# Loading a 1 MB weight table from a channel-major layout: 128 rows of 8 KB in place of 2048 runs of 512 B

## The chip, the cores and the metric

The kernel runs on one core of one Trainium2 chip. The metric is the device time of one execution in microseconds (us); lower is better. The median of three runs of the kernel before is 327.18 us (326.92 to 327.31).

## The reference

x holds 64 batches of 128 channels by 2048 time steps in fp32 (1 MB per batch). Each batch has a condition, an integer from 0 to 15, which picks one of 16 weight matrices of 128 x 128. The batch is multiplied by the picked matrix over its channels, and the product is added to the batch.

```
B, C, T = (64, 128, 2048)
S, D = (16, 128)
W = weights[condition]                       # (64, 128, 128)
out = x + jnp.einsum('bct,bcd->bdt', x, W)
```

The weights come as (state, channel, feature), S x C x D, 1 MB in all.

## The kernel before

A batch is one tile: channels on the 128 partitions, 2048 columns. SBUF holds a ring of 16 such tiles (x_ring: RING_TURNS 4 times STEPS 4), the table of all 16 matrices (weight_table, one row of 16 x 128 numbers per channel), four small tiles for the matrices in use (chosen_weights), and the conditions in one row. PSUM holds two products of four banks each. The order is written out by hand: each engine runs its own loop over turns of four batches and steps on semaphores.

- SyncE (SP) loads x, one DMA of 1 MB per batch (L63). It issues four at once; then load k+4 waits until load k has landed (L72, L76), and from the fifth turn on also until the store of batch k-12, which used the same ring tile, has landed (L77).
- ScalarE (ACT) first issues the load of the conditions (L138) and that of the weight table (L140), then stores one batch per DMA (L134). A store waits for the sum of its batch (L133) and for the landing of the store four batches before (L146). So at most four loads and four stores are under way.
- GpSimd (POOL) waits for both the conditions and the whole table (L89, L90). For each batch it reads the condition into a register and copies the picked 128 x 128 block out of the table into one of the four small tiles (L85). From the fifth batch on it waits until the product that used the tile before is done.
- TensorE (PE) waits for the batch and for its weights (L102, L103), and for the sum that frees its half of PSUM, and makes the product with four fp32 matmuls of 512 columns (L105), which the trace shows as eight instructions.
- VectorE (DVE) adds the product to the x tile in place (L127).

In the table load (L140) the partition is the channel. In memory a channel's data lies in 16 places, one per state, each 128 numbers or 512 B long and 64 KB from the next. The function kernel() makes the arrays contiguous on the host and launches.

Of the kernel before, what the change touches and what calls it, by code (L numbers as in the profile page):

```python
# [1 line left out]

# [3 lines left out]

BANK_COLUMNS = 512
PSUM_BANKS = 8
STEPS = 4
RING_TURNS = 4  # L20


def conditioned_residual(nc, x, condition, weights, out):
    fp32 = mybir.dt.float32
    batches, channels, time = x.shape
    states, _, features = weights.shape
    turns = batches // STEPS
    matmuls = time // BANK_COLUMNS
    psum_slots = PSUM_BANKS // matmuls

    with ExitStack() as ctx:
        def sbuf(name, shape, dtype=fp32):
            return ctx.enter_context(nc.sbuf_tensor(name, shape, dtype))

        def sem(name):
            return ctx.enter_context(nc.semaphore(name))

        x_ring = sbuf("x_ring", [channels, RING_TURNS * STEPS * time])
        weight_table = sbuf("weight_table", [channels, states * features])
        chosen_weights = [sbuf(f"chosen_weights{u}", [channels, features]) for u in range(STEPS)]  # L40
        condition_row = sbuf("condition_row", [1, batches], condition.dtype)
        product = ctx.enter_context(nc.psum_tensor("product", [features, psum_slots, time], fp32))


        condition_loaded = sem("condition_loaded")
        table_loaded = sem("table_loaded")
        x_loaded = [sem(f"x_loaded{u}") for u in range(STEPS)]
        out_stored = [sem(f"out_stored{u}") for u in range(STEPS)]

        weights_chosen = sem("weights_chosen")  # L50
        product_done = sem("product_done")
        sum_done = sem("sum_done")

        def ring_column(turn, u):

            return (turn % RING_TURNS) * (STEPS * time) + u * time

        block = ctx.enter_context(nc.Block())

        @block.sync  # L60
        def _(sp):
            def load(turn, u):
                sp.dma_start(x_ring[:, bass.ds(ring_column(turn, u), time)],  # L63
                             x[bass.ds(turn * STEPS + u, 1)].rearrange("b c t -> c (b t)")
                             ).then_inc(x_loaded[u], 16)

            for u in range(STEPS):
                load(0, u)

            with sp.Fori(1, RING_TURNS) as turn:  # L70
                for u in range(STEPS):
                    sp.wait_ge(x_loaded[u], 16 * turn)  # L72
                    load(turn, u)
            with sp.Fori(RING_TURNS, turns) as turn:
                for u in range(STEPS):
                    sp.wait_ge(x_loaded[u], 16 * turn)  # L76
                    sp.wait_ge(out_stored[u], 16 * (turn - RING_TURNS + 1))  # L77
                    load(turn, u)

        @block.gpsimd  # L80
        def _(pool):
            def choose(turn, u):
                state = pool.value_load(condition_row[0:1, bass.ds(turn * STEPS + u, 1)],
                                        min_val=0, max_val=states - 1)
                pool.tensor_copy(chosen_weights[u][:, :],  # L85
                                 weight_table[:, bass.ds(state * features, features)]
                                 ).then_inc(weights_chosen, 1)

            pool.wait_ge(condition_loaded, 16)  # L89
            pool.wait_ge(table_loaded, 16)  # L90
            for u in range(STEPS):
                choose(0, u)
            with pool.Fori(1, turns) as turn:
                for u in range(STEPS):

                    pool.wait_ge(product_done, (turn - 1) * STEPS + u + 1)
                    choose(turn, u)

        @block.tensor
        def _(pe):  # L100
            def multiply(turn, u):
                pe.wait_ge(x_loaded[u], 16 * (turn + 1))  # L102
                pe.wait_ge(weights_chosen, turn * STEPS + u + 1)  # L103
                for m in range(matmuls):
                    last = pe.matmul(product[:, u % psum_slots, m * BANK_COLUMNS:(m + 1) * BANK_COLUMNS],  # L105
                                     chosen_weights[u][:, :],
                                     x_ring[:, bass.ds(ring_column(turn, u) + m * BANK_COLUMNS, BANK_COLUMNS)],
                                     start=True, stop=True)
                last.then_inc(product_done, 1)

            for u in range(STEPS):
                if u >= psum_slots:
                    pe.wait_ge(sum_done, u - psum_slots + 1)
                multiply(0, u)
            with pe.Fori(1, turns) as turn:
                for u in range(STEPS):
                    pe.wait_ge(sum_done, turn * STEPS + u - psum_slots + 1)
                    multiply(turn, u)

        @block.vector  # L120
        def _(dve):
            with dve.Fori(0, turns) as turn:
                for u in range(STEPS):
                    tile = x_ring[:, bass.ds(ring_column(turn, u), time)]

                    dve.wait_ge(product_done, turn * STEPS + u + 1)
                    dve.tensor_tensor(tile, product[:, u % psum_slots, :], tile,  # L127
                                      AluOpType.add).then_inc(sum_done, 1)

        @block.scalar  # L130
        def _(act):
            def store(turn, u):
                act.wait_ge(sum_done, turn * STEPS + u + 1)  # L133
                act.dma_start(out[bass.ds(turn * STEPS + u, 1)].rearrange("b c t -> c (b t)"),  # L134
                              x_ring[:, bass.ds(ring_column(turn, u), time)]
                              ).then_inc(out_stored[u], 16)

            act.dma_start(condition_row[0:1, :], condition.rearrange("(o b) -> o b", o=1)  # L138
                          ).then_inc(condition_loaded, 16)
            act.dma_start(weight_table[:, :].rearrange("c (s d) -> c s d", s=states),  # L140
                          weights.rearrange("s c d -> c s d")).then_inc(table_loaded, 16)
            for u in range(STEPS):
                store(0, u)
            with act.Fori(1, turns) as turn:
                for u in range(STEPS):
                    act.wait_ge(out_stored[u], 16 * turn)  # L146
                    store(turn, u)
            for u in range(STEPS):
                act.wait_ge(out_stored[u], 16 * turns)


# [17 lines left out]
```

## Time and profile before

| | before |
|---|---|
| median of three runs | 327.18 us (326.92 to 327.31) |
| span of the profiled execution | 324.3 us (no other time of this execution is recorded) |
| PE busy | 231.8 us, 71% |
| DVE busy | 146.7 us, 45% |
| POOL busy | 19.0 us, 6% |
| ACT busy | 0.2 us |
| DMA | 135.27 MB, mean 417 GB/s |
| chain that ended last | 90% DMA, line L63 |

The profile is one execution, taken by the hardware profiler. Its page divides the span into 40 equal slices and gives for each the busy share of every engine in tenths (9 is 90% or more), that of the core's 16 DMA engines, and what they moved in GB/s. The DMA queues are q1 (issued by SP, the loads of x) and q10 (issued by ACT: conditions, table, stores). Every DMA also ends in small packets under 512 B, one on each DMA engine. "Landing" is the time from the issue of a DMA to the arrival of all its data. The chain of waits follows the work that ended last backwards, from each step to what released it. Names ending in q (SPq, ACTq) are the sequencers, which issue DMAs and wait.

### The profile page before, as it was taken

Reading aid. Unit: us, or ns where it says so; the run is one execution under the profiler, and the core shown is the slowest. Engines: PE = TensorE matmul, PEld = TensorE weight load, DVE = VectorE, ACT = ScalarE, POOL = GpSimd, SP = SyncE. Lnnn points to the kernel's source line nnn. Section 1 sums busy time; section 2 is a strip of 40 time slices with the busy share of each in tenths; the row PEclk is TensorE's granted clock in tenths of the full one; section 3 lists DMA queues with packets and bytes.
Section 4 is the critical chain, followed back from the end, with each engine's and each line's share of the span. In section 5 each row is a group of like instructions: output and inputs, shape, how many; then the busy total and the mean of one; then the engine's idle time right before and its main releaser. Section 6 shows DMA issues by size and latency. Waiting matters only on the chain.

```text
span 324.3 us, 2750 instructions
## 1 busy us (share of the span) xinstructions
PE 231.8 (71%) x512; PEld 94.7 (29%) x512; DVE 146.7 (45%) x64; ACT 0.2 (0%) x1; POOL 19.0 (6%) x69
## 2 busy tenths in 40 slices
PE   0039999999999867867768768678677687686200
PEld 0014444444444322322322323223223223232000
DVE  0005576676676554453553543534535535435200
ACT  0000000000000000000000000000000000000000
POOL 0010010010000000000000000000000000000000
PEclk9999999999999999999999999999999999999755
DMA  7999999999999999999999999999999999999995
GB/s 282 384 412 420 427 428 426 427 428 426 425 427 427 427 428 426 427 425 429 425 427 428 426 429 425 427 426 429 424 427 428 426 428 427 426 425 428 427 426 234
DMA packets 18962, 135.27 MB, mean 417 GB/s; under 512 B 2066, under 2 KB 2066, under 8 KB 2578
## 3 DMA queue, kind: packets, MB, share of 16 engines
q10 hardware_dynamic: 9746, 68.16, 49.9%
q1 hardware_dynamic: 9216, 67.11, 49.5%
HBM read 68.16 MB, written 67.11 MB: 417 GB/s over the span
## 4 chain that ended last, share of the span: by engine, by line
DMA 90%; PE 1%; SPq 1%; DVE 1%; issue 1%; DVEq 0%
DMA x_ring<-x 90%; PE product L105 1%; SPq L63 1%; DVE x_ring L127 1%; DVEq L127 0%
## 5 line engine op out<-in xcount | busy, mean ns | idle before, releaser
L105 PE MATMUL product<-x_ring,chosen_weights 128*128 (+1 forms) x512 | 231.8, 603 | 70.2 <-POOL chosen_weights L85 66.4
L127 DVE TENSOR_TENSOR x_ring<-product,x_ring 128x2048 f32 x64 | 146.7, 2292 | 157.8 <-PE product L105 157.8
L105 PEld LDWEIGHTS product<-x_ring,chosen_weights 128*128 128x128 f32 x512 | 94.7, 191 | 206.5 <-issue 206.4
L85 POOL COPY chosen_weights<-weight_table 128x128 f32 x64 | 18.8, 293 | 264.0 <-PE product L105 236.0
L140 ACT MOVE_SHAPE weight_table<-weights x1 | 0.2, 160 | 1.4 <-PEq L157 1.4
L157 POOL MEMSET const-float32-0.0<- 128x1 f32 x1 | 0.1, 98 | 0.1
L157 POOL MEMSET const-bfloat16-1.0<- 128x1 bf16 x1 | 0.1, 101 | 0.0
L157 POOL MEMSET const-uint8-127<- 128x1 uint8 x1 | 0.1, 101 | 0.0
L157 POOL MEMSET const-float32-1.0<- 128x1 f32 x1 | 0.1, 98 | 0.0
L157 POOL BASE_LOAD x1 | 0.0, 17 | 0.2 <-issue 0.2
## 6 DMA issues: line engine op xcount, KB each, us to landing
x_ring<-x SPq DMA_DIRECT2D x64, 1024.0 KB, 19.6
out<-x_ring ACTq DMA_DIRECT2D x64, 1024.0 KB, 19.5
condition_row<-condition ACTq DMA_DIRECT2D x1, 0.2 KB
weight_table<-weights ACTq DMA_DIRECT2D x1, 0.5 KB, 18.2
```

The source lines that it names most:

```text
L63: sp.dma_start(x_ring[:, bass.ds(ring_column(turn, u), time)], x[bass.ds(turn * STEPS + u, 1)].rearrange("b c t -> c (b t)")).then_inc(x_l ...
L85: pool.tensor_copy(chosen_weights[u][:, :], weight_table[:, bass.ds(state * features, features)]).then_inc(weights_chosen, 1)
L105: last = pe.matmul(product[:, u % psum_slots, m * BANK_COLUMNS:(m + 1) * BANK_COLUMNS], chosen_weights[u][:, :], x_ring[:, bass.ds(ring_co ...
L127: dve.tensor_tensor(tile, product[:, u % psum_slots, :], tile, AluOpType.add).then_inc(sum_done, 1)
L140: act.dma_start(weight_table[:, :].rearrange("c (s d) -> c s d", s=states), weights.rearrange("s c d -> c s d")).then_inc(table_loaded, 16)
L157: nc = bacc.Bacc("TRN2", target_bir_lowering=False, num_devices=1)
```

## The change

The host transposes the weights to (channel, state, feature) ahead of the launch. The table load in the kernel reads channel c as one row of 16 x 128 numbers, 8 KB, and writes it as one row of weight_table, whose contents are the same as before. Nothing else is altered.

```diff
-    states, _, features = weights.shape
+    _, states, features = weights.shape
...
-            act.dma_start(weight_table[:, :].rearrange("c (s d) -> c s d", s=states),
-                          weights.rearrange("s c d -> c s d")).then_inc(table_loaded, 16)
+            act.dma_start(weight_table[:, :], weights.rearrange("c s d -> c (s d)")
+                          ).then_inc(table_loaded, 16)
...
-        "weights": np.ascontiguousarray(L0_cond_weights),
+        "weights": np.ascontiguousarray(np.asarray(L0_cond_weights).transpose(1, 0, 2)),
```

## Rows read from the trace of the kernel before

**Rows 1.** The page, part 2: busy tenths in 40 slices of the span.
```profile
PE   0039999999999867867768768678677687686200
...
DMA  7999999999999999999999999999999999999995
```

**Rows 2.** The page, part 3: packets, MB, share of 16 engines' span.
```profile
q10 hardware_dynamic: 9746, 68.16, 49.9%
q1 hardware_dynamic: 9216, 67.11, 49.5%
```

**Rows 3.** The chain of waits: share by line, and pieces (start us, us, what).
```profile
by line: DMA x_ring<-x 90.3%; PE product L105 1.1%; SPq L63 0.9%; DVE x_ring L127 0.7%; issue 0.6%; DVEq L127 0.0%
...
60.27 19.68 DMA x_ring<-x
...
80.14 19.66 DMA x_ring<-x
```

**Rows 4.** Windows by stretch; the last columns are DMA share and GB/s.
```profile
core 0: us, PE busy (x) PEld busy (x) DVE busy (x) ACT busy (x) POOL busy (x), PEclk, DMA share, GB/s
4.00:20.00 16.00, 0.00 (x0) 0.00 (x0) 0.00 (x0) 0.00 (x0) 0.00 (x0) 1.00 1.02 394
20.00:28.00 8.00, 6.81 (x12) 3.04 (x13) 1.31 (x1) 0.00 (x0) 1.46 (x5) 1.00 1.02 423
...
40.00:290.00 250.00, 203.52 (x453) 82.90 (x452) 130.63 (x57) 0.00 (x0) 16.43 (x56) 1.00 1.01 427
...
320.00:324.30 4.30, 0.00 (x0) 0.00 (x0) 0.00 (x0) 0.00 (x0) 0.00 (x0) 0.50 0.14 57
```

**Rows 5.** Timeline from 0 to 30 us: start us, us, engine line op.
```profile
1.56 0.83 ACTq L140 DMA_DIRECT2D weight_table<-weights  x1
...
21.19 9.15 PE L105 MATMUL product<-x_ring,chosen_weights 128*128 128x512 f32 x17 [21.19 <-POOL chosen_weights L85]
...
29.01 0.40 ACTq L134 DMA_DIRECT2D out<-x_ring  x1
```

**Rows 6.** The page, part 6: the table's DMA, median us to landing.
```profile
weight_table<-weights ACTq DMA_DIRECT2D x1, 0.5 KB, 18.2
```

**Rows 7.** DMA view from 321 to 323 us: packets, MB, share of 16 engines.
```profile
q10 hardware_dynamic: 6, 0.05, 5.8%
```

**Rows 8.** Line L63: the issues of x loads one by one, 6 to 32 us.
```profile
L63 SPq DMA_DIRECT2D x_ring<-x x1: 363/363/363, 6.1 to 6.1; - x1
...
L63 SPq DMA_DIRECT2D x_ring<-x x1: 343/343/343, 24.6 to 24.6; - x1
...
L63 SPq DMA_DIRECT2D x_ring<-x x1: 343/343/343, 29.6 to 29.6; - x1
L63 SPq DMA_DIRECT2D x_ring<-x x1: 342/342/342, 32.0 to 32.0; - x1
```

**Rows 9.** DMA view from 8 to 18 us: packets, MB, share of 16 engines.
```profile
q1 hardware_dynamic: 410, 3.01, 79.5%
q10 hardware_dynamic: 409, 0.84, 22.7%
```

**Rows 10.** DMA view from 20 to 28 us, loads alone.
```profile
q1 hardware_dynamic: 461, 3.38, 101.5%
```

**Rows 11.** DMA view from 28 to 30 us: the first store, us to landing.
```profile
out<-x_ring ACTq DMA_DIRECT2D x1, 1024.0 KB, 9.1
```

**Rows 12.** Line L63 from 0 to 5 us: the first four x loads.
```profile
DMA to landing us min/median/max: 5.1/9.3/13.8
```

**Rows 13.** DMA view from 32.4 to 33.4 us: the ACT queue's packets.
```profile
q10 hardware_dynamic: 24, 0.20, 46.7%
```

**Rows 14.** The chain of waits from 290 us on: start us, us, what.
```profile
278.37 19.57 DMA x_ring<-x
...
302.14 2.29 DVE x_ring L127
```

**Rows 15.** Line L134 from 290 us on: ns min/median/max, first and last start us.
```profile
L134 ACTq DMA_DIRECT2D out<-x_ring x9: 345/345/346, 290.8 to 314.3; - x9
```

## Prediction

> **What bounds the kernel now.** I began with the page. The share of busy time by slices shows the DMA digit at 9 in nearly every slice and no compute engine near it: PE is full only up to a third of the span and at 6 to 8 after it [rows 1]. The queue table says why: 135 MB pass through, half on the SP queue (the loads of x), half on the ACT queue (the table, then the stores) [rows 2]. The chain that ended last is 90% DMA, and its pieces all look like the row of 19.66 us: an x load that the next load waited for [rows 3]. So the time is the sum of what the 16 DMA engines must carry, as long as they never run dry. The windows confirm it: the DMA share is about 1.0 from 4 us to beyond 290; the rate is 427 GB/s with loads and stores mixed, 423 with loads alone, but only 394 between 4 and 20 us [rows 4]. That last stretch is where the weight table is on its way: issued at 1.56 us, landed 18.2 us later [rows 5, 6].
>
> The tail has a detail that matters for the sum. The windows give 57 GB/s after 320 us [rows 4], and between 321 and 323 us the DMA view counts 6 packets at a share of 5.8% of sixteen [rows 7]: that is one engine of sixteen still at work, the other fifteen done. One engine trails. It also shows in the chain: a four-load step is 80.14 minus 60.27, 19.87 us [rows 3], while four loads and four stores, 8.39 MB, at 427 GB/s [rows 4] are 19.65 us. So the trailing engine loses about 0.2 us in four pairs, and its last packets are the end.
>
> **What the change removes.** Only one transfer is touched: the table's 1 MB. Its bytes, its queue, its place behind the condition row and its partitions stay; the 512 B runs in memory become 8 KB rows, which is the very form of an x load (128 rows, 1024 KB). So its price after is that of an x load. I cost the saving in two ways.
>
> First, by the SP queue, where load k+4 is issued as soon as load k has landed, so that its issues are a clock of landings. The issue at 6.1 us answers the first landing, the one at 24.6 the seventh, that at 29.6 the ninth [rows 8]. The last two stand 5.0 us apart for two loads: one alone costs 2.5. From 6.1 to 24.6 are six landings, 15.0 us at that price, in 18.5 us: the table took 3.5 us of everyone's time. As one more 8 KB-row transfer it takes 2.5. Saving 1.0 us. (Readings of 0.1 us make this plus or minus 0.15.)
>
> Second, by bytes: 16 us at 394 GB/s are 6.30 MB, which at the 423 of the loads alone [rows 4] take 14.9 us. Saving 1.1 us. A little of this is the stream's start, which stays. I take 1.05.
>
> Where the time sits: in the DMA view from 8 to 18 us the ACT queue's 409 packets took 22.7% of 10 us on 16 engines, 89 ns each; these are the table's, of 2 KB (0.84 MB over 409) [rows 9]. Loads alone from 20 to 28 us: 413 packets of 8 KB (461 less the 48 under 512 B) in 101.5% of 8 us, 315 ns each, or 79 ns per 2 KB [rows 10]. The table's own excess is 512 packets times 10 ns over 16 engines, 0.3 us. The rest is in the x packets that lay beside them: 3.01 MB are 367 packets in 79.5% of 10 us, 347 ns against 315 [rows 9, 10], some 0.7 us in these 10 us. So two thirds of the saving rests on the x packets recovering too; this is a rival below.
>
> The Trainium skill, DMA: Bandwidth & Descriptors, section Why small descriptors are slow, gives a fixed 3 cycles beside one cycle per 32 B, and 32 bytes of metadata per descriptor. For 512 B that is an estimate of 3/16 plus 1/16 of the transfer's 2.5 us, 0.6 us, and the sum by it would be 326.6; the trace has more than that (1.05 us), because it also counts what the neighbours lose, and it decides.
>
> **What the change moves.** The table lands sooner. After the change it is a 1 MB transfer with 8 KB rows, issued on the ACT queue while the SP queue is full. The trace has just that: the first store, issued at 29.01 us, landed in 9.1 us [rows 5, 11]. The bounds are an x load into an idle machine, 5.1 us [rows 12], and the table as it is, 18.2 us [rows 6]. I take 9.1, the row in the same situation, so the table lands near 10.7 instead of 19.8 us. Packet counts agree: from 8 to 18 us the two queues moved 409 and 367 data packets [rows 9], one for one, so the table needs 32 turns per engine now and 8 with 8 KB packets.
>
> The Trainium skill, DMA: Bandwidth & Descriptors, section Queues, rings and completion order, says that an engine takes the queues in turn packet by packet; by that rule the table shares with x for 8 packets of each, about 5 us, and the trace agrees with its even counts.
>
> Everything that hangs on the table comes 9.1 us sooner: the copies on POOL, the first matmul (21.19 us), the first sum and the first store (29.01) [rows 5]. This is worth nothing by itself, since the engines that carry the bytes are full meanwhile. What it does is to mix loads with stores earlier. Two small terms follow. The stretch with loads alone shortens by 9 us, at 423 instead of 427: minus 0.08 us. And the mixed stretch, in which one engine trails, grows at both ends: it starts 9 us sooner and, as the next paragraph shows, its last load lands some 5.5 us later, 14.6 us or three pairs, at 0.05 us each: plus 0.15 us. Together plus 0.07.
>
> **The cover that must hold.** Before, ten x loads have landed when the first stores get their first packets: the issue at 32.0 us says that load 9 is in [rows 8], and stores have 24 packets only from 32.4 us on [rows 13]. Each queue then gets half, so this lead of ten stays, and it is why the last load lands at 297.94 us [rows 14], 26.4 us before the end. After, first store packets come 9 us sooner, near 23.4; from 6.1 us on 6.9 transfers fit at 2.5 us, one of them the table, so about seven loads are in. The tail is then some 7.5 stores at 2.45 us, and the last load lands near 303.5. From there the last product and sum took, before, until 302.14 + 2.29 = 304.43, which is 6.5 us after the landing at 297.94 (278.37 + 19.57) [rows 14], so the last sum is ready near 310. The last store is issued when the fourth before it has landed, some 10 us before the end (314.3 of 324.3 [rows 15]), near 313.3. Three microseconds of cover are left, and the DMA engines do not run dry. PE has cover too: 453 instructions, eight to a batch, kept it busy for 203.5 us [rows 4], 3.6 us a batch, against 4.9 for a load and a store.
>
> ACT's issue of the table, 0.83 us [rows 5], may shorten to the 0.34 of an x load [rows 8]. It is worth nothing: ACT's next job is the first store. POOL, PE and DVE run the same instructions; no wait is added.
>
> **The sum.** Profiled span 324.3 us; minus 1.05, plus 0.07: 323.3. The page records no time of the profiled execution apart from its span; the median of the timed runs, 327.18, stands 2.9 us above it, and this foot is outside the change. So 327.18 - 0.98 = 326.2 us, minus 0.3%. The forecast's own band is 325.9 to 326.5.
>
> **Rivals.**
> 1. Only the table's own packets get faster (0.3 us), and the x packets beside them stay at 347 ns, because two transfers read memory side by side then. For: in the trace the larger part sits in them. Against: with loads and stores side by side the rate is 427, not lower. Time 326.9. Chance 11%.
> 2. No gain: the 394 GB/s belongs to the start of the stream, not to run length. Against it stands the fall to 394 and the return to 423 with the table's landing. Time 327.2. Chance 8%. The Trainium skill, DMA: Bandwidth & Descriptors, section Specifications, puts line rate at 512 B and above, which these runs just meet: by that rule there is nothing to save; the trace has 89 ns against 79, so it speaks against the rule, weakly.
> 3. The change does not do what it says, and the transfer is still cut into small packets, 327.2 as well. Chance 3%.
> 4. Slower: the lead gets too short. If the table landed so early that the stores began with three loads in, the last load would land 3 x 2.45 + 1.2, 8.6 us, before the end by bytes, while the last product, sum and a lone store need 6.5 + 5.1, 11.6 us. The DMA engines idle for 3.0 us: 329.2. It decides below a lead of 4.2; I count seven. Chance 5%.
> 5. Faster still: the trailing engine keeps pace when the engines leave the first microseconds in another order, and its lag goes too. It is 0.2 us in four pairs over the 54 pairs of the mixed stretch, 2.7 us at most, of which I count 2.5: 323.7. Nothing in the trace says why it trails. Chance 5%.
> Forecast: 68%.
>
> The range: 325.5 to 327.3 takes in the forecast's band, rivals 1 to 3 and the spread of the runs (326.92 to 327.31), and leaves out rivals 4 and 5 and some edges, under 2 in 10. About 0.2%, 0.65 us, is what a measurement of this kernel can tell from no change. Faster by more: forecast nearly whole, rival 5 and a part of rival 1, 0.72. Within: rivals 2 and 3, most of 1, the forecast's edge, 0.22. Slower: rival 4 and a trifle, 0.06.
>
> **What would show it.** The table's landing about 9 us after its issue instead of 18.2; 128 packets on the ACT queue for it, none of 2 KB; 420 GB/s or more from 6 us on; SP issues 2.5 us apart per transfer, the table counted as one; first store issued near 19.9 us; last load landing near 303.5; DMA share still 1.0 up to 319; ACT's wait at the last stores on stores, not on sums. I would be wrong if the rate beside the table stayed under 400 (rivals 1, 2), if a gap opened before the last store (rival 4), or if the length of the one-engine tail changed by more than some tenths (rival 5).

## The result and the profile after

Over six runs the changed kernel takes 325.69 us in the median (325.26 to 326.08), the kernel before 326.96 us over as many (326.51 to 327.31). The ratio is 0.9965 with a 95% interval of 0.9952 to 0.9978: 0.35% faster, about 1.1 us, with 0.7 to 1.6 us inside the interval. The forecast was 326.2 us and 0.3%.

The windows of the kernel after, in the stretches of [rows 4] (columns: start:end, length, busy time of PE, PEld, DVE, POOL, granted PE clock, DMA share, GB/s):

```profile
4.00:20.00 16.00, 7.73 (x12) 3.33 (x13) 1.32 (x1) 1.48 (x5) 1.00 1.01 426
20.00:28.00 8.00, 8.00 (x20) 3.61 (x19) 5.56 (x3) 0.59 (x2) 1.00 0.97 383
...
40.00:290.00 250.00, 193.01 (x423) 76.29 (x422) 121.96 (x54) 15.99 (x54) 1.00 1.01 427
...
320.00:324.30 4.30, 0.00 (x0) 0.00 (x0) 0.00 (x0) 0.00 (x0) 0.50 0.05 21
```

The stretch that held the table moved 394 GB/s before [rows 4] and moves 426 now. 16 us at 394 are 14.8 us at 426: 1.2 us gained, what the prediction looked for. But the next stretch has lost: 383 GB/s in 8 us, where the kernel before had 423. At 423 the same bytes take 7.2 us, so 0.8 us go here, at a DMA share near 1. 1.2 - 0.8 leaves 0.4 us, and the spans of the two profiles are 324.3 and 323.9. Packet by packet, fifteen of the DMA engines end at 320.9 us before and 320.4 after, and the last packet of the sixteenth ends at 323.3 and 323.0: 0.5 us gained by the fifteen, 0.1 us lost by the one that trails.

The table and what hangs on it, from the page's part 6 and the timeline of the kernel after:

```profile
weight_table<-weights ACTq DMA_DIRECT2D x1, 1024.0 KB, 9.5
```
```profile
11.84 0.29 POOL L85 COPY chosen_weights<-weight_table 128x128 f32 x1 [11.33 <-issue]
12.27 18.21 PE L105 MATMUL product<-x_ring,chosen_weights 128*128 128x512 f32 x36 [12.27 <-POOL chosen_weights L85]
...
21.00 7.16 ACTq L134 DMA_DIRECT2D out<-x_ring  x3
```

It lands 9.5 us after its issue instead of 18.2 [rows 6], the first matmul starts at 12.27 instead of 21.19 us and the first store at 21.00 instead of 29.01 [rows 5]. The clock of landings, the SP issues of L63 one by one:

```profile
L63 SPq DMA_DIRECT2D x_ring<-x x1: 363/363/363, 5.9 to 5.9; - x1
L63 SPq DMA_DIRECT2D x_ring<-x x1: 358/358/358, 10.8 to 10.8; - x1
...
L63 SPq DMA_DIRECT2D x_ring<-x x1: 342/342/342, 23.2 to 23.2; - x1
```

Six landings and the whole table lie between 5.9 and 23.2 us, 17.3 us in place of the 18.5 of [rows 8]. The table now costs 17.3 - 6 x 2.5 = 2.3 us, like any x load; before it was 3.5. From 6 to 9 us the DMA view shows how it shares with x (columns as in [rows 9]):

```profile
q1 hardware_dynamic: 80, 0.66, 51.5%
q10 hardware_dynamic: 80, 0.66, 51.5%
```

One packet for one, 8 KB each, 0.515 x 3 us x 16 engines / 80 = 309 ns a piece on both queues.

The end of the chain of waits:

```profile
284.76 19.60 DMA x_ring<-x
304.36 0.36 issue
304.72 3.71 PE product L105 x8
...
308.56 2.29 DVE x_ring L127
```

The last load lands at 304.36 us where it landed at 297.94 [rows 14]; the last sum is ready at 310.85, and ACT issues the last store at 313.9, which it does when the fourth store before has landed:

```profile
L134 ACTq DMA_DIRECT2D out<-x_ring x7: 345/345/346, 293.5 to 313.9; - x7
```

Three microseconds of cover stand. The single trailing engine is there as in [rows 7]: between 321 and 323 us the ACT queue's row reads (one of the 7 packets is a small one under 512 B)

```profile
q10 hardware_dynamic: 7, 0.05, 5.8%
```

### The profile page after: what moved, and what is told of

The parts are those of the page before. It is cut to its first block, busy times and chain, and to the rows that moved or that the text cites. A ratio compares the mean times of both kernels' runs of the same rounds, so it can differ in the third digit from the quotient of the medians.

```text
span 323.9 us, 2749 instructions
## 1 busy us (share of the span) xinstructions
PE 235.3 (73%) x512; PEld 94.1 (29%) x512; DVE 146.7 (45%) x64; POOL 19.2 (6%) x69
## 4 chain that ended last, share of the span: by engine, by line
DMA 92%; PE 1%; SPq 1%; DVE 1%; issue 1%; DVEq 0%
DMA x_ring<-x 92%; PE product L105 1%; SPq L63 1%; DVE x_ring L127 1%; DVEq L127 0%
## 5 line engine op out<-in xcount | busy, mean ns | idle before, releaser
L105 PE MATMUL product<-x_ring,chosen_weights 128*128 (+1 forms) x512 | 235.3, 607 | 73.1 <-POOL chosen_weights L85 69.3
```

## The experiments

The theory: a run below some length costs the DMA engines time of its own, and the kernel is as long as its DMA work; when the table lands is worth nothing. Against it stood: the gain comes from the earlier first product and store; it was the start of the stream; two loads side by side slow each other; and the small packets, rather than the runs, are what costs. Each kernel was timed in interleaved runs against the kernel before, whose median was 327.01, 326.56 and 326.94 us in the three sets of runs, so the ratios are what to compare.

| kernel | table | ratio to before, 95% interval | median us |
|---|---|---|---|
| changed, again | 8 KB rows | 0.9965 (0.9953 to 0.9977) | 325.72 |
| late table | 8 KB rows, issued at 10.6 us | 0.9962 (0.9950 to 0.9974) | 325.53 |
| 256 B | 4096 runs | 1.0048 (1.0034 to 1.0062) | 328.32 |
| 1 KB | 1024 runs | 1.0002 (0.9985 to 1.0018) | 326.93 |
| 2 KB | 512 runs | 0.9964 (0.9952 to 0.9977) | 325.54 |
| first, 512 B | ahead of x, 2048 runs | 1.0012 (1.0000 to 1.0025) | 326.81 |
| first, 8 KB | ahead of x, 128 rows | 0.9964 (0.9953 to 0.9976) | 325.39 |
| one state | 64 KB alone | 0.9894 (0.9878 to 0.9910) | 323.54 |
| small early store | 8 KB rows | 0.9965 (0.9952 to 0.9978) | 325.82 |
| stores held | 8 KB rows | 0.9955 (0.9941 to 0.9970) | 325.47 |

**The changed kernel again.** No edit.

> The changed kernel once more, for its spread and for a dip that its first profile has at 23 to 25 us (311 and 270 GB/s, just ahead of the first store's packets, which cost about 0.8 us there). Theory (the 512 B runs cost 1.0 us of DMA time): ratio 0.9965 again, 325.3 to 326.0 us. If the dip belongs to the earlier first store, it is back in this profile; if it is chance, it is gone, the profiled span is near 323.2, and it explains part of the spread.

Ratio 0.9965 once more, 325.19 to 325.94 us. The profile has a span of 323.6 and the dip again. So the dip is no accident of one execution; it comes with this kernel.

These runs also correct a number of the prediction. The 11 runs of the kernel before have spans of 324.2 to 325.2 us, seven of them at 325.0 or above, and each run's time is some 2.0 us over its span (327.14 over 325.1, 326.20 over 324.2). The profiled execution of before, span 324.3, was one of the short ones. The prediction set it against the median and read a foot of 2.9 us. Because only the difference was used, the forecast did not suffer.

**When the table lands.** In the changed kernel ACT waits for the third x load before it issues the table:

```diff
+            act.wait_ge(x_loaded[2], 16)
             act.dma_start(weight_table[:, :], weights.rearrange("c s d -> c (s d)")
                           ).then_inc(table_loaded, 16)
```

> The table in 8 KB rows, but ACT issues it only when the third x load has landed, so that it lands near 19.5 us, as in the kernel before, and the first store starts as late as there. Theory (only the DMA engines' time counts): as fast as the changed kernel, ratio 0.996 to 0.997. Rival (the gain comes from the earlier first product and store): no faster than the kernel before, ratio 1.000.

The first copy is at 20.67 us, as late as in the kernel before (20.76), and yet the ratio is 0.9962. The early landing is worth nothing that these runs can tell (the interval is 0.4 us to either side): the gain is DMA time.

**The length of a run.** The host lays the weights out in half states, or in groups of two or four states (4096 runs of 256 B, 1024 of 1 KB, 512 of 2 KB); the table's contents stay. For 2 KB, against the kernel before (the lines that read the sizes are left out):

```diff
-            act.dma_start(weight_table[:, :].rearrange("c (s d) -> c s d", s=states),
-                          weights.rearrange("s c d -> c s d")).then_inc(table_loaded, 16)
+            act.dma_start(weight_table[:, :].rearrange("c (g r) -> c g r", g=groups),
+                          weights.rearrange("g c r -> c g r")).then_inc(table_loaded, 16)
...
-        "weights": np.ascontiguousarray(L0_cond_weights),
+        "weights": np.ascontiguousarray(np.asarray(L0_cond_weights).reshape(4, 4, 128, 128)
+                                        .transpose(0, 2, 1, 3).reshape(4, 128, 512)),
```

> The launch lays the weights out in half states, so that the table is 4096 runs of 256 B. Theory (a cost per run): the excess of 1.0 us at 2048 runs doubles, ratio 1.003, 328.0 us, and the stretch with the table falls well below 390 GB/s. Rival (the stretch is slow because it is the start of the stream, or because two loads read side by side): no change, 1.000.

> The weights in groups of four states, so that the table is 512 runs of 2 KB. Theory (a cost per run): a quarter of the excess is left, ratio 0.9972, 326.2 us. Rival (what costs is the 2 KB packet in which the trace shows the table, whatever runs it is made of): if the packets stay at 2 KB the excess stays whole, ratio 1.000.

> The weights in groups of two states: 1024 runs of 1 KB. So far: 4096 runs of 256 B 1.0048, 2048 of 512 B 1.000, 512 of 2 KB 0.9964, 128 of 8 KB 0.9965. Theory (some 10 ns of an engine's time per run under 2 KB: 1024 runs x 10 ns over 16 engines, 0.64 us left): ratio 0.998, 326.4 us. Rival (line rate from some length on, the cost is gone at once above 512 B): 0.9964, 325.6 us.

256 B is slower than the kernel before by 0.48%, so the start of the stream is not the cause. From 8 KB rows to 512 B runs is 0.0035 of 327 us, 1.15 us for 2048 runs; from 8 KB to 256 B is 0.0083, 2.7 us for 4096 runs. Spread over 16 engines that is 9 and 10.6 ns of an engine's time per run (the first with an interval of 0.7 to 1.6 us, 6 to 12 ns).

The DMA views from 8 to 18 us, first 256 B, then 2 KB runs (q10 is the table, q1 is x; the line above them counts packets by size):

```profile
DMA packets 911, 3.77 MB, mean 377 GB/s; under 512 B 53, under 2 KB 508, under 8 KB 508
...
q1 hardware_dynamic: 456, 3.30, 87.5%
q10 hardware_dynamic: 455, 0.47, 14.7%
```
```profile
DMA packets 893, 4.16 MB, mean 416 GB/s; under 512 B 73, under 2 KB 73, under 8 KB 489
...
q1 hardware_dynamic: 461, 3.31, 78.9%
q10 hardware_dynamic: 432, 0.85, 22.3%
```

With 256 B runs the table comes in 1 KB packets (0.47 MB over 455), four runs to a packet; with 512 B it came in packets of 2 KB [rows 9], four again. With 2 KB runs there are 416 packets of 2 KB in this view (489 less 73), one run in each. The 2 KB packet is thus the same size with four runs in it and with one, and only beside the first kind are the x packets slow: they take 347 ns [rows 9] with four runs, and 0.789 x 10 us x 16 over 404 packets of 8 KB (3.31 MB), 312 ns, with one run. So the size of the packet alone does not account for the loss; the number of runs goes with it. One thing went along with the number and was not held apart: where the runs are shorter they also lie closer together in memory (32 KB apart for 256 B, 64 KB for 512 B, 256 KB for 2 KB).

I had expected a quarter of the excess to be left at 2 KB (0.9972). The ratio is 0.9964, but its interval (0.9952 to 0.9977) takes in both. The windows tell more. The 2 KB kernel from 4 to 20 us:

```profile
4.00:20.00 16.00, 0.47 (x1) 0.50 (x2) 0.00 (x0) 0.51 (x2) 1.00 1.02 415
```

The changed kernel moved 426 GB/s there, so 16 us x 11 / 426 = 0.4 us are lost with 2 KB runs, a third of the 1.2 us of 512 B. For the other two the whole time of the table is read against the kernel with held stores (below), which has 8 KB rows and moves 424 GB/s in both stretches: 1 KB runs give 409 GB/s from 4 to 28 us, 0.85 us lost, and 256 B runs 386 from 4 to 30 us, 2.3 us lost. In the order 256 B, 512 B, 1 KB, 2 KB that is 9, 9.5, 13 and 13 ns of an engine per run: the loss follows the number of runs, down to 2 KB. That the 2 KB kernel is nevertheless as fast as the changed one fits with the dip at the first stores, which it does not have (below).

The time of the 1 KB kernel is not settled. Its ratio of 1.0002 fits neither 0.998 nor 0.9964, and its twelve spans fall into two groups, three from 323.2 to 323.5 us and nine from 324.6 to 325.5. The profiled one is of the lower group. What adds 1.7 us in the other group no profile shows.

**Alone or side by side.** The table is issued on SP's queue ahead of all x loads, in 512 B runs (an edit of the kernel before) and in 8 KB rows (of the changed kernel). The first of the two edits:

```diff
+            sp.dma_start(weight_table[:, :].rearrange("c (s d) -> c s d", s=states),
+                         weights.rearrange("s c d -> c s d")).then_inc(table_loaded, 16)
             for u in range(STEPS):
                 load(0, u)
...
-            act.dma_start(weight_table[:, :].rearrange("c (s d) -> c s d", s=states),
-                          weights.rearrange("s c d -> c s d")).then_inc(table_loaded, 16)
```

> The table in 512 B runs as before, but issued on SP's queue ahead of all x loads, so that its packets have no packets of x beside them. Theory (a cost per run, wherever it lies): b1 is slower than b2 by 1.2 us, as before is slower than the changed kernel, ratio b1 to b2 1.004. Rival (two thirds of the excess come from two transfers side by side): alone the table loses 0.3 us, b1 to b2 1.001.

> The table in 8 KB rows, issued on SP's queue ahead of all x loads; it should land near 5 us and the first store be issued some 5 us sooner than in the changed kernel, with a lead of about five loads in place of seven. Theory (only bytes count, and a lead of 4.2 is enough): 325.7 us, ratio 0.9962. Rival (the lead is already too short and the engines run dry in the tail): a gap in the DMA share near the end and 1 us or more lost, 0.999 or more.

Page, part 6, of the two:

```profile
weight_table<-weights SPq DMA_DIRECT2D x1, 0.5 KB, 6.6
```
```profile
weight_table<-weights SPq DMA_DIRECT2D x1, 1024.0 KB, 4.9
```

The table lands 1.7 us later in small runs with nothing beside it, and the kernels differ by 1.0012 - 0.9964 = 0.0048, 1.6 us. So the cost does not need two loads side by side, and the slow x packets of [rows 9] are best read as the place where the profile books a part of the table's runs. The windows of the 512 B kernel, then the first one of the 8 KB kernel:

```profile
2.00:6.00 4.00, 0.00 (x0) 0.00 (x0) 0.00 (x0) 0.00 (x0) 1.00 0.91 249
6.00:18.00 12.00, 7.46 (x11) 3.26 (x12) 0.72 (x1) 1.28 (x5) 1.00 1.02 417
```
```profile
2.00:6.00 4.00, 0.00 (x0) 0.00 (x0) 0.00 (x0) 0.00 (x0) 1.00 0.89 354
```

While the table passes, 249 GB/s stand against 354. The table in 512 B runs lands at 7.5 us; from 8 to 18 us the x loads run at 423 GB/s.

The 8 KB kernel's first store is issued at 16.1 us, 4.9 us before the changed kernel's. It is as fast as that one (0.9964), so this shorter lead costs nothing that shows. A lead below 4.2 was not tried.

**What the table costs at all.** Only state 0 is loaded and used for every batch; the other 15 blocks are left out, so the output is that of one matrix.

```diff
-                                 weight_table[:, bass.ds(state * features, features)]
+                                 weight_table[:, 0:features]
...
-            act.dma_start(weight_table[:, :], weights.rearrange("c s d -> c (s d)")
+            act.dma_start(weight_table[:, 0:features], weights[:, 0, :]
                           ).then_inc(table_loaded, 16)
```

> What the table costs at all: only the first of the 16 states is loaded (64 KB), and every batch is multiplied by it; the other 15 blocks are left out, so the output is that of one matrix. Theory: 15/16 of a 1 MB transfer at 2.45 us go from the changed kernel, 323.3 us, ratio 0.989, though the table lands a few us sooner and the lead falls to about five. Rival (a shorter lead lets the engines run dry in the tail): 1 us or more above that, 0.992 or more.

0.9894. So fifteen sixteenths of the table cost 0.0071 x 327 = 2.3 us in 8 KB rows, and 0.0106 x 327 = 3.5 us in 512 B runs. For a whole table that would be 2.5 and 3.7 us, beside the prediction's 2.5 and 3.5. The first price stands on like against like: both kernels have the dip of the next paragraphs (303 and 270 GB/s at 21 to 23 us here). The second does not, because the profiles of the kernel before have no dip, so its agreement is weaker than it looks.

**The dip at the first stores.** In the changed kernel the x packets stretch before the first store's packets arrive. Its DMA view from 23 to 25 us:

```profile
q1 hardware_dynamic: 71, 0.58, 93.1%
```

71 packets in 0.931 x 2 us x 16 engines are 420 ns each, against 309. Two kernels were made for it, and the kernel before was profiled once more. The first adds a store of 64 KB once the table has landed; the second lets ACT wait for the fifth sum ahead of its first store:

```diff
+        early_stored = sem("early_stored")
...
+            act.wait_ge(table_loaded, 16)
+            act.dma_start(out[batches - 1:batches, :, 0:features].rearrange("b c t -> c (b t)"),
+                          weight_table[:, 0:features]).then_inc(early_stored, 16)
+            act.wait_ge(early_stored, 16)
```
```diff
+            act.wait_ge(sum_done, 5)
             for u in range(STEPS):
                 store(0, u)
```

> The changed kernel with a small extra store ahead of the others: 64 KB (128 rows of 512 B of the table) into the last batch's place, which its own store overwrites at the end; issued near 11 us, landed before the first true store. In the profiles of five kernels the x packets stretch from about 2 us after the first store's issue, a loss of 0.4 to 0.8 us. If the first write to HBM sets this off, the stretch comes near 13 us and the first true store has none; if stores of full size do, it stays at 22 to 25 us. If the small store takes the loss away, 325.1 us, ratio 0.9945; if not, its own 0.2 us is added, 325.8 us, 0.9967.

> The changed kernel, but ACT issues no store before the fifth sum, near 35 us, so that loads run alone longer and the lead grows to about twelve. In profiles without the stretch of slow x packets the first store was issued at 29 us or later. If the hour of the first store decides it, there is none here, and the time is 0.4 to 0.8 us less than the changed kernel's, ratio 0.994 to 0.995. If it is the 8 KB table, the stretch comes near 37 us and the ratio stays 0.9965. Theory (the hour of the first store is worth nothing by itself) takes no side beyond that.

> The kernel before once more, one look. The timed runs of before have spans of 325.0 us mostly and 324.2 to 324.5 at times; the profiled one had 324.3. If the dip at the first store (0.8 us in the changed kernel's profiles, none in the profile of before) is what separates them, this profile has a span of 325.0 with a dip to about 300 GB/s near 31 us, or one of 324.3 without. If the dip belongs to 8 KB tables, there is none whatever the span.

The windows with the dip, of the small early store and of the held stores:

```profile
24.00:26.00 2.00, 2.00 (x6) 0.95 (x5) 0.87 (x2) 0.00 (x0) 1.00 0.89 307
```
```profile
38.00:40.00 2.00, 2.00 (x6) 0.95 (x5) 0.86 (x2) 0.00 (x0) 1.00 0.94 369
```

The small store leaves the dip where it was, so a first write as such does not set it off; its ratio is that of the changed kernel. Holding the stores moves the dip with the first store, which is issued at 35.2 us, and makes it shallower (2 us at 369 GB/s cost 0.3 us). Its ratio of 0.9955 overlaps 0.9965, so no gain is shown. The second profile of the kernel before has a span of 324.6 and no dip:

```profile
20.00:28.00 8.00, 6.76 (x10) 2.95 (x11) 0.36 (x1) 0.00 (x0) 1.17 (x4) 1.00 1.01 419
28.00:40.00 12.00, 12.00 (x29) 5.32 (x28) 8.63 (x4) 0.00 (x0) 1.18 (x4) 1.00 1.01 425
```

Is it the early hour of the first store? The profiles speak against that. Here are the late table's kernel, whose first store is issued at 30.1 us, and the 2 KB kernel, whose first store is issued earlier, at 27.3:

```profile
32.00:35.00 3.00, 3.00 (x8) 1.33 (x7) 1.87 (x2) 0.29 (x1) 1.00 1.01 369
```
```profile
28.00:32.00 4.00, 4.00 (x11) 1.85 (x10) 2.55 (x2) 0.29 (x1) 1.00 1.00 412
```

The first loses 0.4 us in its dip, the second 0.1 us at most. What does sort all thirteen profiles is what the ACT queue had carried ahead of the first full store. With no more than 256 data packets (128 for the 8 KB table and for one state, 256 with the small early store, none with the table on SP's queue, in 8 KB rows and in 512 B runs alike) there is a dip, of 0.3 to 0.9 us. With 512 or more (2 KB, 512 B twice, 1 KB, 256 B) there is none to speak of. No kernel was made to test this, and why it should be so stays open.

Neither does the dip explain why executions of the kernel before spread from 323.9 to 325.3 us. Of the 0.3 us between its two profiles (324.3 and 324.6) all lies with the trailing engine: the other fifteen end at 320.9 and 320.8 us, its last packet at 323.3 and 323.6. The two profiles of the changed kernel (323.9 and 323.6) are alike in this: 320.4 and 320.5 us for the fifteen, 323.0 and 322.6 for the last packet.

## Why the prediction was right

**The bound.** Right. The late table shows that the DMA engines' time counts and the table's landing does not. The 2 KB kernel agrees: its table lands 16.7 us after its issue, and its ratio is that of the changed kernel.

**The saving on the table, 1.05 us.** Right in place and near in size. The windows give 1.2 us and the SP issues 1.2 (18.5 against 17.3). The timed ratios give 1.15 (0.7 to 1.6) for the whole change, the dip included. Of the two estimates the one by bytes, 1.1, was nearer, and I had shaded it down for the stream's start.

**The landing, 9.1 us.** Measured 9.5. The first store as nearest row was a good choice. The first store itself came at 21.0, not 19.9 us: 0.2 from the landing (10.9 instead of 10.7), and 0.9 because the first sum follows the first matmul by 6.4 us (12.27 to 18.68) instead of 5.5 (21.19 to 26.69), a difference I did not look for. In the timelines PE starts its first weight loads 0.85 us or more apart and the later ones 0.43; after the change the long steps last 5.2 us (12.24 to 17.45), before it 3.4 (21.16 to 24.60). This costs nothing here.

**The small terms, plus 0.07 us.** The trailing engine's share of them, 0.15 us, is near what the profiles show (0.1). Here a term was missing: the 0.8 us that the profile after loses at 20 to 28 us. Nothing in the trace of before shows it. By the two profiles alone the forecast would have been more than twice too large: their spans differ by 0.4, not 1.0. The timed medians differ by 1.27 us: the profiled execution of before was a short one, and that of the changed kernel (323.9, where the runs have 323.2 to 324.1) a long one. So the forecast of -0.98 came out near the median for a sum that had one term too few, and was measured against a typical execution that the profile did not show. The mechanism and the term for the table hold; the agreement to a few tenths is partly luck. If the table saves 1.2 us and the dip takes 0.8, 0.4 us is left; the timed 1.15 us (0.7 to 1.6) has some 0.7 us more, whose cause is not shown. The trailing engine can hold a part of it, since its lag alone moves by 0.3 to 0.4 us between two profiles of one kernel.

**The cover.** Right: seven loads in when the stores' packets begin, last load at 304.36 (303.5 forecast), last sum at 310.85 (310), last store issued at 313.9 (313.3), cover of 3 us.

**The rivals.** 1, only the table's own packets: fell, b1 against b2. 2, no gain: fell by the 256 B kernel and by the changed one. With it fell the rule of the Trainium skill, DMA: Bandwidth & Descriptors, section Specifications, that 512 B is enough for line rate: by the SP issues 512 B runs cost 3.5 us per table and 8 KB rows 2.3, and in the windows even 2 KB runs lose 0.4 us. The same page's section Why small descriptors are slow points the right way; the estimate of 0.6 us worked out from it is half of what the windows show. 3, the change does not do what it says: the packets are 8 KB. 4, a short lead: not reached, and not tried below 4.2. 5, the trailing engine: it trails as before, 2.6 us behind the fifteen against 2.5.

## What to carry to other kernels

In a kernel whose DMA engines are full all the time, price a change of layout by the DMA time of that one transfer, read as the difference in the landings of what shares the queues with it; when it lands, and what starts sooner, is worth nothing while the engines stay full. Each separate run cost 9 to 13 ns of an engine here, from 256 B to 2 KB: 1.2 us for 1 MB in 512 B runs, 0.4 us in 2 KB runs. Two kernels can have the same time for different reasons, as those with 2 KB and 8 KB have, so read the stretch in question beside the ratio. Compare the profiled span with the spans of the timed runs before you trust a sum to tenths: executions of the same kernel differ here by 1 us.

## What had not been expected

- The x packets stretch from 309 to 420 ns some 2 us after the first store's issue, for 2 to 3 us. It ends at about the time at which that store's own packets come (25.0 us in the changed kernel). This costs 0.4 to 0.9 us where the stores begin at 16 to 21 us, 0.3 to 0.4 where they begin at 30 or 35 us behind an 8 KB table, and nothing in the two profiles of the kernel before. It goes with few packets on the ACT queue before, not with the hour. The cause is open.
- A 2 KB packet shows nearly the same duration with one run in it and with four (0.223 x 10 us x 16 / 416 is 86 ns, against 89); most of what four runs cost seems to be booked on the neighbouring queue's packets (347 against 312 ns).
- A table in 1 KB runs has executions of 323.2 to 323.5 and of 324.6 to 325.5 us, side by side on one chip.
- One DMA engine of the sixteen trails at the end, before and after alike (by 2.5 and 2.6 us; 2.8 in the second profile of before). Why is open.
